# Gated cross-attention block with routed experts: the residual added in TensorE's product, and the output product moved ahead of two weighted-value steps

## The reference

```python
x = x + tanh(g_xattn) * attention(layernorm(x), ctx, ctx)   # rope, 16 heads, softmax, then out @ Wo.T + bo
n = rms_norm(layernorm(x)); probs = softmax(n @ w_router.T); c, ids = top-2 of 8 experts
y_e = (val_e(n) * silu(gate_e(n))) @ w_down_e.T
x = x + tanh(g_ffn) * (sum over the two experts of c * y_e + layernorm(x))
```

## Time and profile before

| | us |
|---|---|
| median of 3 runs | 434.19 (433.54 to 435.53) |
| the profiled execution | 435.61 |
| its span, first to last instruction | 433.8 |
| TensorE busy | 391.3 (90%) |
| weight loads busy (beside TensorE's products) | 267.6 (62%) |
| VectorE busy | 302.5 (70%) |
| ScalarE busy | 260.1 (60%) |
| GpSimd busy | 244.8 (56%) |

### The profile page before, as it was taken

One profiled execution on the slowest core, in us unless ns is written; L12 is line 12 of the kernel. 1 busy time (PEld: TensorE's weight loads), 2 busy tenths in 40 slices (PEclk: granted clock), 3 DMA queues, 4 the chain that ended last, 5 costly groups with the idle time before them and its releaser, 6 DMA issues.

```text
span 433.8 us, 13431 instructions
## 1 busy us (share of the span) xinstructions
PE 391.3 (90%) x3876; PEld 267.6 (62%) x3877; DVE 302.5 (70%) x1167; ACT 260.1 (60%) x582; POOL 244.8 (56%) x201
## 2 busy tenths in 40 slices
PE   8997888999889888988998899998999999999991
PEld 3445454565656545555655578686777878778771
DVE  5878878898898978979786565568655555555550
ACT  3518577786967768676756665644455555454540
POOL 7073233135665555745343367888887458876663
PEclk9999999999999999999998999999999999999997
DMA  7525152353867914325101324544454334444320
GB/s 198 157 60 137 28 133 67 88 145 108 223 162 206 217 55 111 102 58 132 52 29 47 98 59 78 92 65 98 78 76 59 50 48 57 62 52 57 34 24 0
DMA packets 57423, 39.08 MB, mean 90 GB/s; under 512 B 8819, under 2 KB 55158, under 8 KB 57366
## 3 DMA queue, kind: packets, MB, share of 16 engines
q1 hardware_dynamic: 43622, 28.87, 26.1%
q0 software_dynamic: 12736, 8.64, 14.2%
q10 hardware_dynamic: 1008, 0.85, 0.8%
HBM read 14.26 MB, written 11.75 MB: 60 GB/s over the span
## 4 chain that ended last, share of the span: by engine, by line
PE 50%; DVE 17%; DMA 11%; issue 7%; SPq 6%; ACT 4%; POOLq 2%; POOL 1%; DVEq 0%; ACTq 0%
PE bank L1614 9%; PE bank L1592 7%; PE bank L1594 7%; DMA out<-ys,yi 5%; DVE nmx L847 5%; DMA ks<-parts 4%; PE bank L1604 4%; SPq L249 4%; PE bank L1374 3%; PE bank L1401 2%; PE bank L1348 2%; SPq L282 2%; PE bank L1316 2%; PE bank L1317 2%; ACT pt L580 2%
## 5 line engine op out<-in xcount | busy, mean ns | idle before, releaser
L516 POOL DMA_INDIRECT out<-ys,yi x72 | 111.8, 1553 | 43.5 <-issue 23.0
L427 POOL DMA_INDIRECT slots_dram<-xr,slu x64 | 65.5, 1024 | 75.0 <-ACT onT L593 55.1
L847 DVE TENSOR_REDUCE nmx<-bank 128x4 f32<-128x512 f32 x128 | 81.7, 680 | 4.3 <-PE bank L1348 4.3
L580 ACT ACTIVATE pt<-bank 128x512 f32<-128x512 f32 x128 | 72.5, 595 | 9.3 <-PE bank L1361 8.2
L1614 PEld LDWEIGHTS bank<-wf_sb,hT 128*128 128x128 f32 (+1 forms) x432 | 56.9, 190 | 22.7 <-issue 18.0
L1200 DVE TENSOR_TENSOR hh<-sg,bank 128x352 f32<-128x352 f32 x72 | 37.4, 520 | 47.9 <-ACT sg L714 27.2
L1614 PE MATMUL bank<-wf_sb,hT 128*128 (+1 forms) x432 | 61.0, 277 | 4.7 <-DVE hT L1210 4.6
L722 ACT ACTIVATE ys<-bank,yc 128x128 f32<-128x128 f32 x72 | 26.5, 368 | 64.0 <-PE bank L1614 60.1
L1592 PE MATMUL bank<-wf_sb,xT 128*128 x144 | 55.2, 465 | 0.1
L1594 PE MATMUL bank<-wf_sb,xT 128*128 x144 | 54.3, 459 | 0.0
L1374 PE MATMUL bank<-pt,v 128*9 128x128 f32 x1024 | 49.4, 276 | 3.7 <-ACT pt L580 2.5
(11 more groups left out here) (193 smaller groups left out, 707.9 us busy)
## 6 DMA issues: line engine op xcount, KB each, us to landing
qs<-parts SPq DMA_DIRECT2D x48, 128.0 KB
ks<-parts SPq DMA_DIRECT2D x45, 128.0 KB
xs<-slots_dram SPq DMA_DIRECT2D x72, 66.0 KB
wf_sb<-in_wup SPq DMA_DIRECT2D x8, 352.0 KB
x_sb<-in_x SPq DMA_DIRECT2D x8, 256.0 KB, 3.7
ctx_sb<-in_ctx_in SPq DMA_DIRECT2D x8, 256.0 KB, 4.5
out<-x_sb SPq DMA_DIRECT2D x8, 256.0 KB, 2.5
out<-ys,yi POOLq DMA_INDIRECT x72, 3.4
```

What stands on the lines that cost most here:

```text
L427: nc.gpsimd.indirect_dma_start(out=slots_dram, out_offset=bass.IndirectOffsetOnAxis(ap=slu[:, c % 2, k, kk:kk + 1], axis=0), in_=xr[:, c % ...
L516: nc.gpsimd.indirect_dma_start(out=out.rearrange("b s d -> (b s) d"), out_offset=bass.IndirectOffsetOnAxis(ap=yi[:, r:r + 1], axis=0), in_ ...
L580: nc.scalar.activation(pt[:, 4 * g:4 * g + 4, :], STB[g % 2][:, :].rearrange("p (h s) -> p h s", h=4), ACT.Exp, scale=SCORE_SCALE).then_in ...
L847: nc.vector.tensor_reduce(nmx[:, b % 2, at:at + 4], SB[g % 2][:, :].rearrange("p (h s) -> p h s", h=4), AX.X, ALU.max, negate=True).then_i ...
```

## The change

- `project_out` multiplies with `wog`, which is `wo_sb` times tanh(g_xattn), made once by ScalarE behind `values(0)`. The bias rows get the same factor by one more VectorE instruction at the start.
- A third product goes into the same accumulation: the unit matrix, in float32, with `x_sb[:, b, :]`. The result in PSUM is then the whole new x.
- `add_attention` on VectorE is gone. ScalarE copies the sum to `x_sb` in a new step `residual(b - 1)`, the last of each pass of its loop. Signal `a_x1` takes the place of `d_x1` for all who waited.
- In TensorE's loop `project_out(b - 1)` moves from the end, behind `transpose_maximum(b + 2)`, to ahead of `weighted_values(b, 2)`.
- For the last batch `residual(B - 1)` stands behind the first `gate` of the tiles.

```diff
+            def residual(b):
+                act.wait_ge(pe_o, b + 1)
+                nc.scalar.activation(x_sb[:, b, :], SMALL[:, D:2 * D], ACT.Copy).then_inc(a_x1, 1)
...
             values(0, SMALL)
+            nc.scalar.activation(wog[:, :], wo_sb[:, :], ACT.Identity, scale=tg[:, 0:1]).then_inc(a_wog, 1)
             middle(0, 0)
...
                 if u == 3 and there(c - 1):
                     base(c - 1)
+                if real(b - 1):
+                    residual(b - 1)
...
             rows_up(0, 1)
             nc.scalar.activation(silu_table[:, :], tg[:, 0:1], ACT.Silu)
             gate(0, 0)
+            residual(B - 1)
...
                 bias.link(nc.vector.tensor_tensor(bop[:, 0, :], SB[1][0:3, 0:D], bo_sb[:, :], ALU.add))
+                dve.wait_ge(a_tg, 1)
+                bias.link(nc.vector.tensor_scalar(bop[:, 0, :], bop[:, 0, :], tg[0:3, 0:1], None, ALU.mult))
...
-            def add_attention(b):
-                dve.wait_ge(pe_o, b + 1)
-                dve.wait_ge(a_xh, b // CH + 1)
-                nc.vector.scalar_tensor_tensor(x_sb[:, b, :], SMALL[:, D:2 * D], tg[:, 0:1], x_sb[:, b, :],
-                                               ALU.mult, ALU.add).then_inc(d_x1, 1)
-
             def statistics1(b):
 
-                dve.wait_ge(d_x1, b + 1)
+                dve.wait_ge(a_x1, b + 1)
...
-                if real(b - 1):
-                    add_attention(b - 1)
...
             def project_out(b):
                 pe.wait_ge(a_aT, b + 1)
-                mm(SMALL[:, D:2 * D], onT[:, :], wo_sb[:, :], start=True, stop=False)
-                mm(SMALL[:, D:2 * D], onesb[0:3, :], bop3[:, :], start=False, stop=True).then_inc(pe_o, 1)
+                if b == 0:
+                    pe.wait_ge(a_wog, 1)
+                mm(SMALL[:, D:2 * D], onT[:, :], wog[:, :], start=True, stop=False)
+                mm(SMALL[:, D:2 * D], onesb[0:3, :], bop3[:, :], start=False, stop=False)
+                mm(SMALL[:, D:2 * D], ident, x_sb[:, b, :], start=False, stop=True).then_inc(pe_o, 1)
...
+                if real(b - 1):
+                    project_out(b - 1)
                 if real(b):
                     weighted_values(b, 2)
                     weighted_values(b, 3)
                 if real(b + 2):
                     transpose_maximum(b + 2)
-                if real(b - 1):
-                    project_out(b - 1)
```

More of the change, by code:

```diff
@@ L105, in flamingo @@
         wo_sb, bo_sb, bop = sb("wo_sb", [128, 128]), sb("bo_sb", [3, 128]), sb("bop", [3, 2, 128])
+        wog = sb("wog", [128, 128])
         bhigh, bop3 = sb("bhigh", [3, 3, 128], BF16), sb("bop3", [3, 128], BF16)
@@ L200, in flamingo @@
             sem, ("a_tg", "a_xh", "a_xT", "a_exp", "a_aT", "a_xn", "a_nT", "a_e"))
-        d_max, d_mT, d_rc, d_on, d_x1, d_q = map(sem, ("d_max", "d_mT", "d_rc", "d_on", "d_x1", "d_q"))
+        d_max, d_mT, d_rc, d_on, a_x1, d_q = map(sem, ("d_max", "d_mT", "d_rc", "d_on", "a_x1", "d_q"))
         d_stat, d_ve, d_rs, d_stat2, d_ve2, d_t2, d_sc2, d_rt, d_top, d_m12, d_slot, d_sl, d_pr = map(
@@ L206, in flamingo @@
             sem, ("a_oT", "pe_heads", "d_bn", "d_sc", "d_tp", "d_fs", "d_ntg"))
-        d_mx, d_slf = sem("d_mx"), sem("d_slf")
+        d_mx, d_slf, a_wog = sem("d_mx"), sem("d_slf"), sem("a_wog")
         p_rs, p_k, p_rs2 = map(sem, ("p_rs", "p_k", "p_rs2"))
@@ L1254, in _ @@
                 result_rows(0, r)
-            add_attention(B - 1)
             statistics1(B - 1)
@@ L1289, in keep_busy @@
             def keep_busy(b, n):
-                pe.wait_ge(d_x1, b - 1)
+                pe.wait_ge(a_x1, b - 1)
                 for _ in range(n):
@@ L1410, in transpose_attended @@
                 if b:
-                    pe.wait_ge(d_x1, b)
+                    pe.wait_ge(a_x1, b)
                 nc.tensor.transpose(SMALL[:, 0:D], on[:, :], ident).then_inc(pe_aT, 1)
@@ L1493, in _ @@
             pe.wait_ge(d_zero, 5)
-            pe.wait_ge(d_bo, 8)
+            pe.wait_ge(d_bo, 9)
             pe.wait_ge(d_rq, 1)
@@ L1645, in _ @@
             up(0, 1, first[1])
-            pe.wait_ge(d_x1, B)
+            pe.wait_ge(a_x1, B)
             transpose_hidden(0, 0)
```

## The result

| | before | after |
|---|---|---|
| median | 434.19 us (433.54 to 435.53) | 450.66 us (446.87 to 454.21, 4 runs) |
| ratio | 1 | 1.033, 95% interval 1.027 to 1.039 |
| profiled execution, span | 435.61, 433.8 | 446.87, 445.1 |
| VectorE busy | 302.5 | 291.3 |
| ScalarE busy | 260.1 | 266.6 |

The change makes the kernel 3.3% slower, by the ratio some 14.3 us. The ratio leaves out the run of 454.21 us, which was in a slower state of the chip, so it is not the quotient of the two medians (1.038). The four runs after had granted clocks of 0.985, 0.964, 0.985 and 0.966 and took 446.87, 454.21, 449.56 and 451.77 us, so part of their spread goes with TensorE's clock; the profiled one is the fastest. The profiled execution before had 0.991.

A forecast was written before the change was run, and what follows sets the result against it. No engine was full; a serial chain of waits, half TensorE, was taken as the bound. Six chunks (2.4, 3.3 and 3.0 us by pairs), batches 26 to 28 (1.3) and the end (+0.2) gave +10.2: 444.5 us, range 437.5 to 449.5.

The forecast's parts named there:

- Added pair and block: Output product on TensorE: the unit-matrix product's two passes plus a pause add 0.43 us, growing the block from 0.58 to 1.01.
- Batch 2's tail: End of a chunk's batch 2, from the copy of the attended rows to the next batch: +0.38 us.
- Batches 3 and 0: Their tails: block delays transposed maxima; +0.51 us in batch 3, in batch 0 +0.74 by the queue or +0.43 by VectorE.
- Batch 1 costs 0: Tail of a chunk's batch 1: grows likewise, but under the landing of the stacked keys, so 0.
- ScalarE's copy: Copy of the sum, last in ScalarE's loop: bounds 0 to 0.28 us a batch, 0.20 taken in two chunks through ScalarE.
- The end: End of attention, fillers waiting for the residual: 0, -0.6, +0.4, and last sum +0.4; together +0.2 us.
- the pair streams: Rival: no new pauses from pair to weighted values or maxima to next batch; about +5 us, 439.5 us; chance 0.15.
- VectorE as the bound: Rival: dropping VectorE's add gains 0.31 us at each of some 12 crossings, 3.7 us; 430.5 us; chance of faster 0.08.
- ScalarE as the bound: Rival: ScalarE's copy delays heads in batches 0 and 1 of seven chunks, 3.9 us more; 448.5 us; chance 0.09.

The follow-up runs named there:

- maxima-early run: The changed kernel with the transposed maxima directly behind the output product, ahead of weighted values 2 and 3; ratio to the kernel before 1.011.
- late-scores run: The changed kernel with the second part of the scores moved behind the heads' transposes; ratio to the kernel before 1.035.
- copy by VectorE: The changed kernel with the sum copied to x_sb by VectorE at its old place, not by ScalarE; ratio to the kernel before 1.041.
- pair only: The changed kernel with the output product moved back behind the transposed maxima, keeping the unit-matrix pair and ScalarE's copy; ratio to the kernel before 1.008.
- move only: The kernel before with the output product moved ahead of weighted values 2 and 3, VectorE still adding; ratio to the kernel before 1.024.

## Why the prediction was right and where not

The direction, the mechanism and the block were right. On the profiled execution the sum said 445.8 us and it took 446.87. On the median it said 444.5 (434.19 and 10.2 are 444.4); the ratio of 1.033 makes it 448.5, within the range, and the plain median of 450.66 is 1.2 us above the range, with two of the four runs at granted clocks of 0.964 and 0.966. So the size was 10.3 where 14.3 came.

That the sum lies within 1.1 us of the profiled execution is in part luck, for two misses cancel. By the transposed maxima of the two traces the kernel after is 0.5 us late at the first full chunk (51.78 against 51.28), where I had 0; 11.6 late six chunks on (222.93 against 211.29), so 11.1 for what I had at 8.7; 13.0 late at the last ones (1.4 where I had 1.3); and 11.3 late at the end of the span, so the end gives back 1.8 where I had it cost 0.2.

- *Added pair and block.* Taken 0.43 and 1.01; the trace has 0.42 and 1.00. That TensorE pauses behind the pair was taken from other rows, and held. Right here, but not at every change between kinds of product, as I had it: between the pair and the transposed maxima the maxima-early run has no pause (105.35 to 105.56), nor had the kernel before between the transposed maxima and the output product (104.18 and 104.19).
- *Batch 2's tail.* +0.38 forecast, 1.81 against 1.46 found, +0.35. Right.
- *Batches 3 and 0.* Maxima late, VectorE idle some 0.8 ahead of its copies: found 0.79 to 0.95 and, over 60 to 250 us, 28.4 us in 26 waits against 6.9 in 12. Right in kind, too small in what follows, next point.
- *Batch 1 costs 0, and the move's cost is the block alone: this step failed.* The chunk shown took 2.22 us more, where I had at most 1.63; the mean of six is 1.86 where I had 1.45. Starts of the transposed maxima give it by batch, worked out from the two traces (from 96.75 us before and 99.82 after, a little off the windows above):

```
interval to the transposed maxima issued in   batch 2  batch 3  batch 0  batch 1   chunk
before                                          7.43     6.56     6.89     6.04    26.92
after                                           8.16     7.42     7.20     6.38    29.16
```

  Batch 1, where I had 0, has 0.34. Two waits are missing from the sum. The scores' second part waits for `maximum_low`: from the first load of scores by key to the heads' transposes it is now 1.15 us (108.19 to 109.34), where it was 0.78. And the query projection of batch 2 waits for a rotation that is late with batch 1's maxima. I had named who waits for the transposed maxima as VectorE's copies and SyncE's queue, and left out TensorE itself, by way of the shared bank. The late-scores run shows that the first wait is not a cost by itself: lifted, nothing is gained. How much of the 2.4 us that the six chunks took beyond my sum each wait makes up was not measured (0.7 of it is clock, below).
- *ScalarE's copy.* Taken 0 in batches 2 and 3: in the trace it starts at 107.53 and 115.97, and what follows has other waits. Right; the copy by VectorE was no better. The 0.20 that I took in two chunks no run isolates.
- *The end.* Taken +0.2, found -1.8: the shift of the last transposed maxima was 13.0 us and that of the first expert tiles 11.1. The fillers at 256.32 come 11.2 later against 10.8 for those at 250.69, the +0.4 that I gave, and the last sum likewise. The gain before them is larger than my 0.6, some 2.3 us: the stretch at 1.2 GHz around 231.44 is gone, which I had left at 0 with a bound of 1.3. Another of 3.4 us appeared at 152.1, where one batch takes 7.09 us for 6.38, so 0.7 of the loss in the chunks is clock:

```profile
152.13:155.54 3.41, 3.41 (x32) 2.52 (x27) 3.31 (x20) 1.65 (x4) 2.54 (x2) 0.50 1.09 250
```

- *The rest of the gap*, 446.87 to the median, is between runs of one kernel. Two of the four have the lower clock and the longer times, but the two at 0.985 still differ by 2.7 us; why was not tried, and on the other chips the kernel before has such a spread as well.

The rivals: the pair streams (no pauses) is refuted by 107.01 to 107.43. VectorE as the bound is refuted by pair only, which relieves VectorE the same and is no faster (1.008, where this rival wanted 431 us or less, 0.993). ScalarE as the bound is refuted by the copy by VectorE, which takes that work from ScalarE and is no faster (1.041).

## What to carry to other kernels

Taking work off an engine pays only if what feeds that engine does not come later; ask of a moved step not how long it is but who waits for what it is now ahead of, its own engine included when two tensors share a bank. When two edits come together, run each alone: here the move was some 70% of the loss, while the pair, put into an existing wait, cost nothing that could be told. A small product of another shape or type in a serial tail can cost more by its pauses than by its passes: without the bias product the block was 0.36 us shorter, of which its pass would be 0.06. And when a sum comes out right, compare it stage by stage: here 3.0 us too little and 2.0 too much stood in it.

## What the runs showed of the hardware

- TensorE's pause between products depends on the two kinds that meet. Behind a float pair of 128x128 and ahead of the bias row or the weighted values it is 0.20 us (0.42 from load to load, where a second pair follows 0.22 behind the first). From the load of the 3-row bf16 product to the next it is 0.16, pass included. From a float pair to the next pair, or to the float transpose of 16 columns, there is none (0.22 and 0.21).
- On the three new chips the signal of a small transpose came late in some batches: VectorE's copy behind it starts up to 1.13 us after its load (move only), where the first chip has 0.32 in all but one batch of the changed kernel's trace (0.52) and two of the kernel before (0.52 and 0.64). The cause is open.
- The same kernel took 434 us on one chip and 444 to 449 us on three others. On two of the four chips the trace of the kernel before is at hand: 0.991 and 0.967 of the full clock, with one stretch at 1.2 GHz of 3.4 us before the end against five of 3.4 to 6.8 us.
